# Attention stage of an early-fusion kernel: TensorE's units taken in turn, and the exponential over all logits ahead of VectorE's first replacement

## The reference, cut to what matters

```
def _L0_ffn_ref(x, ...):                       # x: (4, 640, 128), HEADS 8, TOPK 16
    x = x + (depthwise_conv3(x) + pos_b)
    q, k, v = split(x @ qkv_w.T + qkv_b)       # 8 heads of 16 channels
    logits = einsum('bmd,bpd->bmp', q * scale, k)
    _, idx = lax.top_k(logits, 16)
    attn = softmax over the 16 chosen logits
    out = einsum('bmk,bmkd->bmd', attn, v[idx])
    return out @ wo_w.T + wo_b
h = h + _L0_ffn_ref(_layernorm(h), ...)
```

## Time and profile before

| | |
|---|---|
| median of 3 runs | 6033.43 us (6028.88 to 6035.36) |
| profiled execution, its own time | 6077.31 us |
| its span in the profile | 6075.6 us |
| mean granted clock of PE over the span | 0.894 |
| busy share of the span | PE 63%, VectorE 91%, ScalarE 55%, GpSimd 74% |
| attention stage | from about 5305 us to the end, some 770 us |

### The profile page before, as it was taken

The page is one execution under the profiler, slowest core; times in us unless marked ns, Lnnn a source line. Parts: engine busy times, 40 slices in busy tenths (PEclk is TensorE's granted clock), DMA queues, the critical chain, the costliest instruction groups (busy, mean ns, idle before and its releaser), DMA issues. The chain is left out here.

```text
span 6075.6 us, 59026 instructions
## 1 busy us (share of the span) xinstructions
PE 3857.0 (63%) x13520; PEld 2181.2 (36%) x13520; DVE 5508.9 (91%) x7805; ACT 3318.1 (55%) x5826; POOL 4516.4 (74%) x3041
## 2 busy tenths in 40 slices
PE   2433223266767767667677676776767766588888
PEld 1222112233433334333333333333433333266666
DVE  6888788579999999999999999999999999777688
ACT  2323213256666666666666666666666665544455
POOL 7004402269999999999999999999999999633344
PEclk7766667689999999999999999999999999877688
DMA  1000000134444444444444444444444444200000
GB/s 29 1 13 1 1 0 12 38 136 171 172 168 170 169 168 173 168 170 168 169 172 169 169 168 171 169 171 167 169 171 168 169 168 171 98 2 2 2 3 3
DMA packets 172980, 695.44 MB, mean 114 GB/s; under 512 B 28455, under 2 KB 36120, under 8 KB 172632
## 3 DMA queue, kind: packets, MB, share of 16 engines
q1 hardware_dynamic: 168262, 687.87, 31.0%
q0 software_dynamic: 1536, 3.14, 0.2%
q10 hardware_dynamic: 2834, 0.66, 0.1%
HBM read 685.04 MB, written 6.55 MB: 114 GB/s over the span
## 5 line engine op out<-in xcount | busy, mean ns | idle before, releaser
L914 POOL TENSOR_TENSOR m_hs<-m_u,m_BC 128x1280 f32<-128x1280 f32 x1024 | 2999.1, 2929 | 72.2 <-DVE m_u L1295 72.2
L1145 PE MATMUL m_PS<-m_pr,ident 128*128 128x512 f32 (+1 forms) x6144 | 2444.2, 535 | 845.3 <-DVE m_pr L1269 844.9
L1261 DVE TENSOR_TENSOR_SCAN m_hs<-m_PS,m_hs 128x640 f32<-128x640 f32 x2048 | 2956.7, 1470 | 12.5 <-ACT m_PS L971 6.7
L1145 PEld LDWEIGHTS m_PS<-m_pr,ident 128*128 128x128 f32 x6144 | 1111.4, 191 | 2077.9 <-DVE m_pr L1269 1076.3
L971 ACT ACTIVATE m_PS<-m_dt,m_A 128x640 f32<-128x640 f32 x2048 | 1613.0, 793 | 429.6 <-DVE m_hs L1261 403.1
L921 POOL TENSOR_TENSOR m_pr<-m_hs,m_BC 128x384 f32<-128x384 f32 x1024 | 1056.0, 1031 | 93.5 <-DVE m_hs L1261 91.5
L1269 DVE TENSOR_TENSOR m_pr<-m_hs,m_PS 128x896 f32<-128x896 f32 x1024 | 1081.7, 1056 | 4.7 <-DVE m_hs L1261 4.2
L324 POOL TENSOR_TENSOR g_prod<-g_hbuf,g_E 128x128 f32<-128x128 f32 x592 | 246.3, 453 | 763.3 <-ACT g_E L388 745.9
L960 ACT COPY m_PS<-m_BC 128x448 f32<-128x448 f32 x1024 | 548.2, 535 | 427.3 <-DVE m_u L1295 83.1
L426 PE MATMUL g_TB<-ident,g_nrm 128*128 128x128 f32 x200 | 65.7, 329 | 437.2 <-DVE g_nrm L580 427.3
L393 ACT ACTIVATE g_rstd<-g_rstd 128x100 f32<-128x100 f32 x6 | 1.7, 286 | 569.9 <-DVE g_rstd L684 569.9
(11 more groups left out here) (249 smaller groups left out, 4398.0 us busy)
## 6 DMA issues: line engine op xcount, KB each, us to landing
m_BC<-m_scr SPq DMA_DIRECT2D x1024, 640.0 KB, 3.7
m_scr<-m_CB SPq DMA_DIRECT2D x32, 160.0 KB, 4.2
m_hs<-in_cwr SPq DMA_DIRECT2D x4, 512.0 KB, 4.0
out<-f_res SPq DMA_DIRECT2D x20, 64.0 KB, 1.5
m_inw<-in_in_w SPq DMA_DIRECT2D x4, 256.0 KB, 4.0
m_dtw<-in_dw SPq DMA_DIRECT2D x4, 256.0 KB, 3.8
m_xw<-in_xw SPq DMA_DIRECT2D x8, 64.0 KB, 3.8
m_outw<-in_ow SPq DMA_DIRECT2D x4, 128.0 KB, 3.5
```

What stands on the lines that cost most here:

```text
L914: pool.tensor_tensor(hs[:, g % RH], u[:, p % 2], BC[:, g % UB:g % UB + 1, 0:S].to_broadcast([P, DT, S]), ALU.mult).then_inc(w_ready, 1)
L1145: ins = pe.matmul(Y[:, a:e], ident[:], pr[:, g % RP, a:e], start=False, stop=False, skip_group_check=True)
L1261: v.tensor_tensor_scan(hs[:, g % RH, d, :], half[d], hs[:, g % RH, d, :], 0.0, ALU.mult, ALU.add).then_inc(scan_done, 1)
```

## The change

It has four parts.

1. PE's list. Round n was: transposes of `old` and `old+1`, `pv(old)`, logits of `2n+2` and `2n+3`, `pv(old+1)`. It is now, for q = 0 and 1: logits of `2n+2+q`, transposes of `old+q`, `pv(old-2+q)`. So `pv` comes one pair later than the transposes.
2. `probT` has four slots for two, so `probT_copy(c)` waits for `pv` of unit c-4 and not c-2.
3. ScalarE's list. Round n was: copy, `exp_all`, copy, `exp_all`, `exp_cut`, `exp_cut`. It is now: `exp_all`, `exp_all`, copy of `old`, `exp_cut`, `exp_cut`, copy of `old+1`. `exp_all` no longer waits for VectorE's first replacement.
4. VectorE's first replacement now waits for `exp_all` of the same unit. `finish_a`, `finish_b`, `o_out` and `o_copy` come one round later, and the loop has one round more (`LONG`).

GpSimd's and SyncE's lists are unchanged.

```diff
-    LONG = PAIRS + 5
+    LONG = PAIRS + 6
-        probT = sb("probT", [P, 2, TILES, P])
+        probT = sb("probT", [P, 4, TILES, P])
@@ ScalarE
                     def probT_copy(c):
-                        if c >= 2:
-                            act.wait_ge(pv_done, b * UNITS + (c - 1))
+                        if c >= 4:
+                            act.wait_ge(pv_done, b * UNITS + (c - 3))
                     def exp_all(c):
                         act.wait_ge(neg_ready, b * UNITS + (c + 1))
-                        act.wait_ge(cut1_ready, b * UNITS + (c + 1))
                     for n in range(LONG):
-                        for q in range(2):
-                            if 2 <= n < PAIRS + 2:
-                                probT_copy(2 * (n - 2) + q)
-                            if n < PAIRS:
-                                exp_all(2 * n + q)
+                        old = 2 * (n - 2)
+                        if n < PAIRS:
+                            exp_all(2 * n)
+                            exp_all(2 * n + 1)
+                        if 2 <= n < PAIRS + 2:
+                            probT_copy(old)
                         if n < PAIRS:
                             exp_cut(2 * n)
                             exp_cut(2 * n + 1)
+                        if 2 <= n < PAIRS + 2:
+                            probT_copy(old + 1)
@@ PE
                     for n in range(LONG):
                         old = 2 * (n - 2)
-                        if 2 <= n < PAIRS + 2:
-                            transposes(old)
-                            transposes(old + 1)
-                            pv(old)
-                        if n + 1 < PAIRS:
-                            logits(2 * n + 2)
-                            logits(2 * n + 3)
-                        if 2 <= n < PAIRS + 2:
-                            pv(old + 1)
+                        for q in range(2):
+                            if n + 1 < PAIRS:
+                                logits(2 * n + 2 + q)
+                            if 2 <= n < PAIRS + 2:
+                                transposes(old + q)
+                            if 0 <= old - 2 + q < UNITS:
+                                pv(old - 2 + q)
@@ VectorE
                         for c in two:
                             v.wait_ge(top_ready, g0 + (c + 1))
+                            v.wait_ge(exp_ready, g0 + (c + 1))
                             v.match_replace(cut1[:, c % 2, :], top1[:, c % 4, :], LG[:, c % 2, 0:S], CUT)
```

More of the change, by code:

```diff
@@ L1508, in probT_copy @@
                     def probT_copy(c):
-                        k = c % 2
                         act.wait_ge(probT_ready, b * UNITS + (c + 1))
-                        if c >= 2:
-                            act.wait_ge(pv_done, b * UNITS + (c - 1))
-                        act.copy(probT[:, k].rearrange("p j q -> p (j q)"), PT[:, 0:S]).then_inc(probT_copied, 1)
+                        if c >= 4:
+                            act.wait_ge(pv_done, b * UNITS + (c - 3))
+                        act.copy(probT[:, c % 4].rearrange("p j q -> p (j q)"), PT[:, 0:S]).then_inc(probT_copied, 1)
                     def exp_cut(c):
@@ L1535, in _ @@
                     for n in range(LONG):
-                        if n >= PER + 3 and (n - PER - 3) % PER == 0:
-                            o_copy((n - PER - 3) // PER)
-                        for q in range(2):
-                            if 2 <= n < PAIRS + 2:
-                                probT_copy(2 * (n - 2) + q)
-                            if n < PAIRS:
-                                exp_all(2 * n + q)
+                        if n >= PER + 4 and (n - PER - 4) % PER == 0:
+                            o_copy((n - PER - 4) // PER)
+                        old = 2 * (n - 2)
[4 more added lines that the diff above has]
+                            probT_copy(old)
                         if n < PAIRS:
@@ L1602, in pv @@
                     def pv(c):
-                        t, hd, k = c // HEADS, c % HEADS, c % 2
+                        t, hd = c // HEADS, c % HEADS
                         pe.wait_ge(probT_copied, b * UNITS + (c + 1))
@@ L1607, in pv @@
                         for j in range(TILES):
-                            ins = pe.matmul(Ov[:, hd, :], probT[:, k, j, :], vp[:, j, hd, :],
+                            ins = pe.matmul(Ov[:, hd, :], probT[:, c % 4, j, :], vp[:, j, hd, :],
                                             start=(j == 0), stop=(j == TILES - 1))
@@ L1625, in _ @@
                     for n in range(LONG):
-                        if n >= PER + 3 and (n - PER - 3) % PER == 0:
-                            o_out((n - PER - 3) // PER, 1)
-                        old = 2 * (n - 2)
-                        if 2 <= n < PAIRS + 2:
-                            transposes(old)
-                            transposes(old + 1)
-                            pv(old)
-                        if n + 1 < PAIRS:
-                            logits(2 * n + 2)
-                            logits(2 * n + 3)
-                        if 2 <= n < PAIRS + 2:
-                            pv(old + 1)
-                        if n >= PER + 2 and (n - PER - 2) % PER == 0:
-                            o_out((n - PER - 2) // PER, 0)
+                        if n >= PER + 4 and (n - PER - 4) % PER == 0:
+                            o_out((n - PER - 4) // PER, 1)
+                        old = 2 * (n - 2)
+                        for q in range(2):
[5 more added lines that the diff above has]
+                                pv(old - 2 + q)
+                        if n >= PER + 3 and (n - PER - 3) % PER == 0:
+                            o_out((n - PER - 3) // PER, 0)
                         if b + 1 < B and 0 <= n - PAIRS < 4:
@@ L1735, in _ @@
                             v.match_replace(cut1[:, c % 2, :], top1[:, c % 4, :], LG[:, c % 2, 0:S], CUT).then_inc(cut1_ready, 1)
+                        if n >= PER + 3 and (n - PER - 3) % PER == 0:
+                            finish_a((n - PER - 3) // PER)
+                        if n >= PER + 5 and (n - PER - 5) % PER == 0:
+                            finish_b((n - PER - 5) // PER)
                         for c in two:
```

## The result

The changed kernel takes 6462.83 us (median of 4 runs, 6458.2 to 6468.38) against 6034.4 us before (its median with a fourth run; 6033.43 with three): a ratio of 1.0706 with a 95% interval of 1.0685 to 1.0727, 428 us slower. The forecast was 6417 us with a range of 6275 to 6475. The profiled execution took 6465.4 us with a span of 6463.7, which is 388 us over the span before.

A forecast was written before the change was run, and what follows sets the result against it. PE was taken to bound the attention stage, level with VectorE at full clock. 68 rounds x (13.1 - 7.515) = +380 us, plus 4 for the ends, on 6033.4 gave 6417 us; range 6275 to 6475.

The forecast's parts named there:

- The ring: Closed chain of waits through PE, GpSimd, ScalarE and VectorE each round: 9.6 us at full clock, 13.8 at half.
- handing over: Four passes between engines in each round of the ring, 0.1 to 0.8 us in all, taken as 0.4.
- VectorE's new wait: First replacement waits for exp_all: 0.9 us a round within the ring, some 0.6 us if ScalarE were free.
- The clock: PE loses full clock in each round's pause and regains it late or not at all: 13.1 us a round.
- the Trainium skill's rule: Array throttled by default, activity releases it: all 68 rounds at 13.8 us, 6465 us, with 0.2 of the forecast's 0.75.
- the fall at 5607: PE's clock level fell there after a round busy 1.12 of 2.00 us around the copy; half clock for 16.4 us.
- The forecast of 0.5 to 0.6 for the mean: PE's granted clock in the attention stage was to fall from 0.79 to 0.5 to 0.6.
- First pairs and ends: Pairs 0 to 2 taken as nothing; the extra round at item ends 0 to 16 us, taken as 4.
- From the profiled execution to the median: Profiled execution before lay 44 us above the median, taken as untouched by the change: 6461 became 6417 us.
- A: Rival: the ring holds but PE's clock stays high for much of it, 6179 to 6274 us; chance 0.16.
- B: Rival: the ring is looser and only VectorE's new wait costs, 0.6 us in 68 rounds, 6075 us; chance 0.03.
- C: Rival: no ring, PE runs through without its stop for the copy, 6.5 us a round, 5964 us; chance 0.05.

The follow-up runs named there:

- The filler: The changed kernel with four more fp32 matmuls of 256 columns at the end of PE's rounds 3 to 19, in its pause: 10.43 us a round, 6299.49 us.
- Each cut: The changed kernel with four slots of prob (8.75 us a round), without VectorE's new wait (10.22), or with four slots of e_cut (10.66).
- the second profile: The kernel before, unchanged, profiled once more on another chip: 7.02 us a round, items at 8.20, 6.62, 6.62 and 6.62.
- the two kernels with and without it: The kernel before with VectorE's new wait alone (9.28 us a round, 6232.89 us), and the changed kernel without that wait (10.22, 6313.75 us).
- the ring cut: The changed kernel with four slots of prob and without VectorE's new wait: 7.12 us a round, 6084.89 us, ratio to before 0.9986.
- work at the round's end: The kernel before with one more fp32 matmul of 256 columns at the end of PE's rounds 3 to 19: 7.06 us a round, ratio 0.9985.
- the filler in the stop: The kernel before with one fp32 matmul of 256 columns between a pair's transposes, where PE stands for ScalarE's copy: 6038.87 us, ratio 0.9906.

## Why the prediction was right, point by point

**The ring.** Right, in its links and nearly in its length. At half clock I had 13.8 us, the chain has 13.63 with the last transposes partly at full clock; handing over was taken at 0.4 and is 0.40. The filler shows it at full clock, 9.59 for 9.6. Each cut moved the round as expected, 8.75 for 8.5, 10.22 for 10.4, 10.66 for 10.6; the mix of the two clocks within each of these was a guess.

**VectorE's new wait.** The size given for it within the ring, 0.9 us, was too small: undoing it took 3.0 us off a round. The ring's sum alone does shrink by 0.9; the rest I read as clock, since the mean granted clock of the stage is 0.76 without the wait and 0.63 with it, but that part wasn't separated.

**The clock.** Right in its direction, and in its size only as a mean. I took five sixths of the way to half clock, 13.1 us, for every round; the mean round is 13.27, but of two kinds. The windows of item 1, the first three rounds from pair 2 and then the other fourteen:

```profile
5640.81:5673.71 32.90, 20.07 (x94) 15.05 (x94) 19.00 (x37) 13.16 (x19) 10.31 (x13) 0.79 0.00 0
5673.71:5865.50 191.79, 139.84 (x545) 108.41 (x546) 90.07 (x177) 60.78 (x88) 47.75 (x56) 0.62 0.01 2
```

The three take 10.97 us each at a granted clock of 0.79, the fourteen 13.70 at 0.62, since these get full clock for some 3 us only, which lie in the pause. So steady rounds stand at the half-clock sum of 13.8, and the mean is lower through the rounds at an item's start, which the prediction didn't tell apart. The filler in the pause shows that it was the clock. The chain has every steady round of item 1 begin at half clock, with logits of 2.50 us. That is what the Trainium skill's rule gave (TensorE: Matmul & The Clock Gate, What's actually happening: throttled by default, released by activity). That its 6465 us for the medians was nearer than my 6417 is luck: on the profiled execution the same sum is 6077.3 + 431.4 = 6509 us, and 6465.4 was measured.

The prediction took the fall at 5607 as a sign that a fall follows a stop. Both profiles of before have items with the same stop of 0.86 us in every round and a granted clock of 1.00 throughout, so the stop alone doesn't bring the fall.

The forecast of 0.5 to 0.6 for the mean was a little low (0.63), that of 200 us more idle time on PE a little high: 721 - 592 = 129 before, 1104 - 787 = 317 after, +188.

**First pairs and ends.** Taken as +4, measured -8.5 (10.6 and 1.8 shorter, 4.0 longer). The last is the two products behind the last transposes, 3.9 in the prediction; that the passages got shorter wasn't foreseen. The stage begins 5.3 us later, which no part of the change explains; before's own profiles, on two chips, differ by more.

**From the profiled execution to the median.** On the profiled execution the sum gave 6461 us and it took 6465.4. So near a hit is partly luck: the rounds were 11.5 us more than forecast, the first pairs and ends 12.5 less, and the stage began 5.3 later. On the medians it gave 6417 and 6463 was measured, and this is where the 46 us are. I had subtracted the 44 us between before's profile and its median as something that the change doesn't touch. They sit, at least in part, in the rounds: the first profile had two items at 8.03 and 8.79, which are 17 x (1.41 + 2.17) = 61 us over four items at 6.62. A run of before can be that much shorter; the changed kernel has no such items. The mean of 7.515 that went into the sum was a chance value of one execution; with the 7.02 of the second profile the sum on the medians would be 34 us more, 6451.

**The rivals.** A (mostly full clock) fails by the 0.63 and by 13.27. B (only the wait, 0.6 us a round) fails by the two kernels with and without it. C (no ring) fails for the change as it is. With the ring cut, PE's round without the stop for the copy gained nothing (6084.89 us, ratio 0.9986). Its idea that the falls of before come from that stop stays open: work in the stop ends them, but work at the round's end does so too.

## What to carry to other kernels

When an order is rewritten, write down for each buffer which operation frees its slot and what now stands ahead of that on its engine, and follow it round until it closes: the sum of such a ring is a floor for the round, and a look at who waits now won't show it, since the ring doesn't exist yet. Two slots more in the right buffer can be worth more than the order (13.27 to 8.75 us here). Where PE stops for another engine in every round, a small matmul in that stop is worth a try: here it cost no time, the granted clock stayed up and the kernel ran 0.9% faster, while the same matmul at the round's end gave its gain back.

## What the runs showed of the hardware

One and the same program had two kinds of items, 6.62 us a round at a granted clock of 1.00 and 8 to 9 us at 0.74 to 0.81, and not the same ones in its two profiles; its 29 runs on one chip spread over 53 us. One matmul of 0.43 us a round, a fifteenth of it, made all four items equal to 0.05 us in 113. And a kernel that loses the clock in every steady round is as steady as one whose rounds hold it: the changed kernel's four runs lie within 10 us and those of the filler in the stop, six on another chip, within 9. Its steady rounds repeat at 13.6 to 13.9 us with full clock in the same 3 us of each, where PE has least to do.
